# Second MLP product on one core: the last chunk's 42 rows, high and low half stacked in one tile, two matmuls in place of three

## The chip, the core and the metric

The kernel runs on one core of one Trainium2 chip. The metric is the device time of one execution in microseconds (us). The kernel before takes 3081.09 us, the median of three runs (3079.54 to 3083.18). The core's engines are named as in the profile: PE is TensorE (PEld its weight loads), DVE is VectorE, ACT is ScalarE, POOL is GpSimd, SP is SyncE, which issues the DMAs. Every engine runs its own instruction stream, and the streams meet at semaphores.

## The reference

The input x has shape (4, 2048, 256). Two blocks follow each other, each with a residual and layer norms:

```python
x = x + layernorm(attention(layernorm(x)))     # softmax over axis 1, full attention of each batch
x = x + layernorm(transformer(layernorm(x)))   # two layers, windows of 128 tokens
# one layer: x += local_attention(shift(x) @ wqkv, 8 heads of 64) @ wo
#            h  = layernorm(shift(x)) * g + b
#            a, g = split(h @ w1 + b1, 2)      # HID = 682 columns each
#            x += (a * gelu(g)) @ w2 + b2      # w2 is 682 x 256
```

The change concerns the last line, the product with w2. Its contraction runs over HID = 682 = 5 x 128 + 42 values.

## The kernel before

The function `phase_a` computes the first block (up to about 650 us of the profile). `phase_b` starts with a stage that loads and splits the weights (about 651 to 729 us) and then runs both layers as one stream of 128 windows of 128 tokens, 64 of layer 0 and 64 of layer 1. Each engine has a function `run(s, r, pairs, layer)` that issues its work of slot `s`; in a slot, different windows are in different steps. Most slots stand in two hardware loops of four slots, the first slots of each layer and the last ones are written out. The order of the work is written by hand in these functions; nothing reorders it.

The MLP is done for two windows at a time, a pair. In an even slot (`r % 2 == 0`) PE computes the product with w1 (L1000). ACT applies the gelu (L1101), DVE multiplies (L1238) and leaves `hid`, in 6 chunks of up to 128 hidden values (on the partitions) by 256 tokens. Only 42 partitions of the last chunk, number FULL = 5, are used. To get more than 16-bit precision out of 16-bit products, POOL splits each chunk: `hid_hl[:, 0]` is the value rounded to float16 (the high half, L1253), `hid_hl[:, 1]` the rest (the low half, L1255). It does four chunks at the end of the even slot and the last two in the odd slot, in the middle of its other work. w2 is split in the same way before the stream starts. In the odd slot PE computes the product with w2 (L1012): for each of two windows and each of 6 chunks three matmuls of 256 columns, given by `PARTS`: high by high, high by low, low by high. That is 36 matmuls a pair, and 64 pairs. The unused partitions of the last chunk hold zeros (L1338).

What stands around this on each engine:

- PE, after the w2 product, turns q and k of the next window (L903, L910), computes the qkv product (L925), then turns the softmax weights of the window before (L941, 16 transposes) and multiplies them with v (L953), then computes scores (L966), the output product (L979), and in even slots the w1 product (L1000). In an even slot L941 waits for `xpp` (L1156), DVE's reading of the w2 product. L953 waits for ACT's copies of the turned weights (L1068).
- DVE, in the odd slot, takes the scores (L1204), then normalises the 8 heads' weights (L1216), heads 0 to 3, then the low half of the next input (L1112), then heads 4 to 7. In the next slot come the low halves of q and k (L1181, L1183), the statistics of the layer norm (L1140, L1143), then `xpp` (L1156) and the rotary terms (L1125, L1126).
- POOL, in the odd slot: layer norm helpers (L1272 to L1277), the squares (L1281), the last two chunks of `hid_hl` (L1253, L1255), then qr and the sum for kr (L1289, L1291), inverse norms (L1295, L1297), kr (L1301), the inverse norm of q (L1305), xb (L1310), the low half of the layer norm's output (L1262), and in layer 1 the final sum (L1333). When the next slot is the first of a group of four, a mask copy (L1268) follows.
- ACT, in the even slot, makes the normalised input (L1039, L1041) from POOL's `shift2` (L1277), which comes from DVE's L1143, and only after it the copies L1068.

The constant `SECOND_REST` is 64, the first partition of the upper half of a tile.

Of the kernel before, what the change touches and what calls it, by code (L numbers as in the profile page):

```python
# [21 lines left out]
ALU = mybir.AluOpType  # L22
# [5 lines left out]
P = 128  # L28
# [4 lines left out]
LAYERS, HEADS, DH = 2, 8, 64  # L33
INNER = HEADS * DH
HP = HEADS // 2
HID = int(D * 4 * 2 / 3)
FULL = HID // P
REST = HID - FULL * P
HC = FULL + 1

W1_BLOCKS = 2 * FULL + 1
SECOND_REST = P // 2
# [20 lines left out]
LAST_SLOT = NT + 6  # L63
FILL_GROUPS = 2
PARTS = ((0, 0), (0, 1), (1, 0))
HID_EARLY = 4
W1_BANKS = (0, 1, 6, 3, 4, 5)
BANK_READ = {3: 3, 4: 4, 5: 7, 6: 8}
# [438 lines left out]
def phase_b(nc, w, consts, x2_dram, xs_dram, xp_dram, rot_dram, out):  # L507
# [9 lines left out]
    with ExitStack() as keep:  # L517
# [9 lines left out]
        w2 = sb("w2", [P, LAYERS, 2, HC, D], F16)  # L527
# [9 lines left out]
        with ExitStack() as ctx:  # L537
# [14 lines left out]
            w2_f = sb("w2_f", [P, LAYERS, HC, D])  # L552
# [4 lines left out]
            bias_sq, low = sb("bias_sq", [P, LAYERS]), sb("low", [P, 3, LAYERS])  # L557
# [8 lines left out]
            step, scale_ready, w1_hi, w2_hi, bias_added = sem("step"), sem("scale_ready"), sem("w1_hi"), sem("w2_hi"), sem("bias_added")  # L566
            loaded_mlp = sem("loaded_mlp")
            block = ctx.enter_context(nc.Block())
            DMAS_ROT, DMAS_MLP, DMAS = 1 + 6, LAYERS * 5 + 1, 4

            @block.sync
            def _(sp):
# [11 lines left out]
                for l in range(LAYERS):  # L584
                    sp.dma_start(w2_f[:, l, 0:FULL, :], w["w2"][l, 0:FULL * P, :].rearrange("(c p) d -> p c d", p=P)).then_inc(loaded_mlp, 16)
                    for first_block, first_row, half in ((0, 0, 0), (HC, SECOND_REST, HID)):
# [1 line left out]
                                     allow_slow_non_contiguous=True).then_inc(loaded_mlp, 16)  # L588
                        sp.dma_start(b1_f[first_row:first_row + REST, l, FULL:HC], w["b1"][l, half + FULL * P:half + HID].rearrange("(p c) -> p c", c=1),
                                     allow_slow_non_contiguous=True).then_inc(loaded_mlp, 16)  # L590
                sp.dma_start(w2_f[0:REST, :, FULL, :], w["w2"][:, FULL * P:HID, :].rearrange("l p d -> p l d")).then_inc(loaded_mlp, 16)

                sp.dma_start(rot_all[:, (LAYERS - 1) * WPB:LAYERS * WPB, :], consts["rot"]).then_inc(loaded_rot, 16)
                for n, name in enumerate(("q_scale", "k_scale")):
# [136 lines left out]
        with ExitStack() as ctx:  # L731
# [33 lines left out]
            hid = sb("hid", [P, HC, 2 * P])  # L765
            hid_hl = sb("hid_hl", [P, 2, HC, 2 * P], F16)
# [26 lines left out]
            w1_done, gelu_done, hid_ready, hid_hi, hid_lo = (sem(n) for n in ("w1_done", "gelu_done", "hid_ready", "hid_hi", "hid_lo"))  # L793
# [4 lines left out]
            vk_cleared = sem("vk_cleared")  # L798
# [88 lines left out]
            def _(pe):  # L887
# [7 lines left out]
                def run(s, r, pairs, layer):  # L895
# [88 lines left out]
                    j = pairs - 2  # L984
# [19 lines left out]
                    if r % 2 == 1 and in_range(2 * j):  # L1004

                        pe.wait_ge(hid_lo, HC * (j + 1))
                        if in_range(s - 1):
                            pe.wait_ge(scores_kept, HEADS * (s - 1) + BANK_READ[3])
                        for n in range(2):
                            for c in range(HC):  # L1010
                                for a, (hp, wp) in enumerate(PARTS):
                                    last = nc.tensor.matmul(ps[:, 3, n * D:(n + 1) * D], hid_hl[:, hp, c, n * P:(n + 1) * P],  # L1012
                                                            w2[:, ds(layer(2 * j), 1), wp, c, :],
                                                            start=(c == 0 and a == 0), stop=(c == HC - 1 and a == 2))
                        last.then_inc(w2_done, 1)

                transpose_hx(0, 0)
# [227 lines left out]
            def _(pool):  # L1245
                def hid_halves(j, first, end):

                    if in_range(2 * j):
                        wait(pool, w2_done, j)
                        for c in range(first, end):  # L1250
                            rows = slice(0, P if c < FULL else REST)
                            wait_apart(pool, hid_ready, HC * j + c + 1, passed_pool)
                            nc.gpsimd.tensor_copy(hid_hl[rows, 0, c, :], hid[rows, c, :]).then_inc(hid_hi, 1)  # L1253
                            pool.wait_ge(hid_hi, HC * j + c + 1)
                            nc.gpsimd.tensor_tensor(hid_hl[rows, 1, c, :], hid[rows, c, :], hid_hl[rows, 0, c, :], ALU.subtract).then_inc(hid_lo, 1)  # L1255

                def input_low(t):
                    if in_range(t):
# [76 lines left out]
                nc.gpsimd.memset(v[:], 0.0).then_inc(vk_cleared, 1)  # L1335
                nc.gpsimd.memset(kT[:].bitcast(F32), 0.0).then_inc(vk_cleared, 1)
                nc.gpsimd.memset(kT_low[:].bitcast(F32), 0.0).then_inc(vk_cleared, 1)
                nc.gpsimd.memset(hid_hl[:, :, FULL, :], 0.0).then_inc(vk_cleared, 1)  # L1338
                slots(pool, run)


# [57 lines left out]
```

## Time and profile before

| | |
|---|---|
| median of three runs | 3081.09 us |
| the profiled execution's own time | 3083.64 us |
| its span, first to last instruction | 3081.9 us |
| PE busy | 2908.2 us (94%) |
| PE weight loads busy | 2508.8 us (81%) |
| DVE busy | 2481.2 us (81%) |
| POOL busy | 2070.3 us (67%) |
| ACT busy | 2038.6 us (66%) |
| mean granted TensorE clock | 0.978 of full speed |

The profile is one execution. PE's busy time counts a matmul until its modelled end, so that matmuls overlap in it; the weight loads (PEld), of which there is one for each matmul, show better when PE had nothing to do. DVE's and POOL's instructions are shown with start and duration in us. An idle time in brackets is that of the engine just before the instruction, with what ended it. "Layer 0" in the stream is about 825 to 1995 us by the starts of the w2 products, "layer 1" what follows.

### The profile page before, as it was taken

The page shows a single profiled execution, that of the slowest core. Times are in us where ns is not written, and L with a number is a line of the kernel's source. Part 1 is how long each engine was busy: PE and PEld are TensorE (multiplying, and loading weights), DVE is VectorE, ACT ScalarE, POOL GpSimd, SP SyncE. Part 2 cuts the span into 40 slices and gives each one's busy share as a digit, 9 for nine tenths or more (in the row PEclk, how much of TensorE's full clock was granted, in tenths as well). Part 3 has the DMA queues.
Part 4 walks back from the last instruction along what each step waited for, and adds up shares of the span by engine and source line. Part 5 has one row for each costly group of instructions (what it writes and reads, how often), then busy time and mean ns, then how long its engine had stood idle before and what let it go on. Part 6 is the DMA issues. An engine that isn't in the chain of part 4 may idle for free. (4 is left out here: it accounts for less than half of the span.)

```text
span 3081.9 us, 81609 instructions
## 1 busy us (share of the span) xinstructions
PE 2908.2 (94%) x25720; PEld 2508.8 (81%) x25720; DVE 2481.2 (81%) x6734; ACT 2038.6 (66%) x4644; POOL 2070.3 (67%) x2807
## 2 busy tenths in 40 slices
PE   7999999963999999999999999999999999999996
PEld 4868676753888888888888888888888888888885
DVE  7989888746887888887888888888888888888884
ACT  6253534203777777777777777777777777777774
POOL 0323232124778878778777777888888888888885
PEclk9999999976999999999999999999999999999998
DMA  1211111151111111111111111222121112221221
GB/s 39 62 49 56 55 56 49 47 179 75 49 55 48 51 54 53 53 50 48 52 57 51 54 48 49 56 66 57 56 60 55 54 55 59 65 58 56 59 55 44
DMA packets 273029, 176.92 MB, mean 57 GB/s; under 512 B 95775, under 2 KB 270851, under 8 KB 272515
## 3 DMA queue, kind: packets, MB, share of 16 engines
q1 hardware_dynamic: 272898, 175.24, 19.4%
q8 instruction: 75, 1.23, 0.2%
q14 instruction: 56, 0.45, 0.1%
HBM read 103.82 MB, written 54.54 MB: 51 GB/s over the span
## 5 line engine op out<-in xcount | busy, mean ns | idle before, releaser
L1086 ACT ACTIVATE b_probs<-b_probs,b_negmax 128x256 f32<-128x256 f32 x1024 | 507.9, 498 | 77.2 <-DVE b_negmax L1204 76.5
L925 PE MATMUL b_ps<-b_wqkv,b_hT_hi 128*128 128x512 f32 x1536 | 499.1, 406 | 3.0 <-issue 2.0
L1000 PE MATMUL b_ps<-b_h2T,b_w 128*128 128x256 f16 x4224 | 473.7, 273 | 8.3 <-DMA b_h2T<-b_xh_hl 8.3
L1000 PEld LDWEIGHTS b_ps<-b_h2T,b_w 128*128 128x128 f16 x4224 | 414.0, 98 | 56.9 <-DMA b_h2T<-b_xh_hl 8.6
L1216 DVE TENSOR_SCALAR b_probs<-b_probs,b_rinv 128x256 f32<-128x256 f32 x1024 | 412.8, 466 | 9.0
L457 PE MATMUL a_ps<-a_xn_hl,a_E 128*128 128x256 f16 x3072 | 344.5, 273 | 8.8 <-DVE a_E L323 8.8
L457 PEld LDWEIGHTS a_ps<-a_xn_hl,a_E 128*128 128x128 f16 x3072 | 299.4, 98 | 44.2 <-ACT a_e L402 9.6
L925 PEld LDWEIGHTS b_ps<-b_wqkv,b_hT_hi 128*128 128x128 f32 x1536 | 283.4, 191 | 62.5 <-issue 2.4
L1204 DVE CUSTOM_DVE_ANT_0 b_probs<-b_ps,b_mask,b_rn 128x256 f32<-128x256 f32 x768 | 317.8, 480 | 0.0
L1173 DVE TENSOR_TENSOR b_oT<-b_ps,b_oT 128x512 fp32r<-128x512 f32 x128 | 88.6, 692 | 280.9 <-ACT b_oT L1077 280.9
L1068 ACT COPY b_probsT<-b_ps 128x512 f32<-128x512 f32 x512 | 261.2, 593 | 80.9 <-PE b_ps L941 80.8
L925 PE MATMUL b_ps<-b_wqkv,b_hT_lo 128*128 128x512 f32 x768 | 306.4, 399 | 0.0
L1255 POOL TENSOR_TENSOR b_hid_hl<-b_hid,b_hid_hl 128x256 f16<-128x256 f32 (+1 forms) x384 | 258.2, 673 | 30.9
L1012 PE MATMUL b_ps<-b_w,b_hid_hl 128*128 128x256 f16 x2304 | 261.9, 273 | 3.0 <-POOL b_hid_hl L1255 3.0
L941 PEld LDWEIGHTS b_ps<-b_ident_f,b_probs 128*128 128x128 f32 x2048 | 230.6, 142 | 39.9 <-issue 20.4
L941 PE MATMUL b_ps<-b_ident_f,b_probs 128*128 128x128 f32 x2048 | 247.5, 274 | 13.8 <-DVE b_xpp L1156 12.4
L953 PE MATMUL b_ps<-b_probsT,b_v 128*64 128x128 f32 x4096 | 256.3, 278 | 3.4 <-ACT b_probsT L1068 1.1
L1012 PEld LDWEIGHTS b_ps<-b_w,b_hid_hl 128*128 128x128 f16 x2304 | 224.8, 98 | 28.9 <-POOL b_hid_hl L1255 3.2
L953 PEld LDWEIGHTS b_ps<-b_probsT,b_v 128*64 128x64 f32 x4096 | 219.0, 136 | 33.4 <-ACT b_probsT L1068 19.9
L1101 ACT ACTIVATE b_gl<-b_ps,b_b,b_w_unit 128x256 f32<-128x256 f32 (+1 forms) x384 | 203.0, 562 | 52.8 <-PE b_ps L1000 39.5
L1305 POOL TENSOR_TENSOR b_rn<-b_ss_min,b_mhalf 128x8 f32<-128x8 f32 x128 | 233.3, 1822 | 0.0
L1238 DVE SCALAR_TENSOR_TENSOR b_hid<-b_ps,b_b1a,b_gl 128x256 f32<-128x256 f32 (+1 forms) x384 | 177.6, 481 | 62.7 <-ACT b_gl L1101 62.7
(164 smaller groups left out, 6830.7 us busy)
## 6 DMA issues: line engine op xcount, KB each, us to landing
b_hx<-xs_dram SPq DMA_DIRECT2D x256, 64.0 KB, 1.9
b_rot<-rot_dram SPq DMA_DIRECT2D x128, 128.0 KB, 2.1
b_xr<-xs_dram SPq DMA_DIRECT2D x128, 128.0 KB, 2.1
xp_dram<-b_xp SPq DMA_DIRECT2D x128, 128.0 KB, 1.7
b_h<-xp_dram SPq DMA_DIRECT2D x256, 64.0 KB, 1.8
a_x_res<-in_L_attn_x_dram SPq DMA_DIRECT2D x64, 128.0 KB, 2.2
x_dram<-a_x SPq DMA_DIRECT2D x64, 128.0 KB, 1.7
xs_dram<-a_xo SPq DMA_DIRECT2D x64, 128.0 KB, 1.8
```

The costliest lines, as they stand in the source:

```text
L457: last = nc.tensor.matmul(ps[:, bank, 0:D], E[:, j, a, i * P:(i + 1) * P], xn_hl[:, b % 2, j, c, :], start=(j == 0 and a == 0 and c == 0), ...
L925: last = nc.tensor.matmul(ps[:, bank, :], hT[:, k, :], wqkv[:, ds(layer(s), 1), part, k, bank * INNER:(bank + 1) * INNER], start=(k == 0 a ...
L941: last = nc.tensor.transpose(ps[:, 3 + p, n * P:(n + 1) * P], probs[:, 2 * p + n // 2, (n % 2) * P:(n % 2 + 1) * P], ident_f[:])
L953: last = nc.tensor.matmul(ps[h * DH:(h + 1) * DH, 7, p * P:(p + 1) * P], v[:, window, (2 * p + h) * DH:(2 * p + h + 1) * DH], probsT[:, p, ...
L1000: last = nc.tensor.matmul(ps[:, bank, half * 2 * P:(half + 1) * 2 * P], w1[:, ds(layer(2 * j), 1), wp, k, first:first + P], h2T[:, hp, k, ...
L1012: last = nc.tensor.matmul(ps[:, 3, n * D:(n + 1) * D], hid_hl[:, hp, c, n * P:(n + 1) * P], w2[:, ds(layer(2 * j), 1), wp, c, :], start=(c ...
L1068: nc.scalar.copy(probsT[:, p, :], ps[:, 3 + p, :]).then_inc(pT_kept, 1)
L1086: nc.scalar.activation(probs[:, h, :], probs[:, h, :], ACT.Exp, bias=negmax[:, h:h + 1], scale=-1.0, accum_out=rowsum[:, h:h + 1]).then_in ...
L1204: nc.vector.tensor_tensor_reduce(probs[:, h, :], head_scores(h), which, rn[:, (r - 1) % 2, h:h + 1], ABOVE_ALL, ALU.add, ALU.min, negmax[: ...
L1216: nc.vector.tensor_scalar(probs[:, h, :], probs[:, h, :], rinv[:, h:h + 1], None, ALU.mult).then_inc(probs_ready, 1)
L1255: nc.gpsimd.tensor_tensor(hid_hl[rows, 1, c, :], hid[rows, c, :], hid_hl[rows, 0, c, :], ALU.subtract).then_inc(hid_lo, 1)
L1305: nc.gpsimd.tensor_tensor(rn[:, r % 2, :], ss_min[:, 0:HEADS], mhalf[:, 0:HEADS], ALU.pow).then_inc(rn_ready, 1)
```

## The change

The last chunk's high half stays on partitions 0 to 41 of `hid_hl[:, 0, FULL]`. Its low half is no longer written to `hid_hl[:, 1, FULL]` but to partitions 64 to 105 of the same tile `hid_hl[:, 0, FULL]`. The last 42 rows of w2 are loaded twice, to partitions 0 to 41 and to 64 to 105, by a DMA more. One matmul over the stacked tile and the weights' high half then gives high by high plus low by high, and one over the weights' low half gives high by low plus low by low, a product that was left out before. The last chunk takes two matmuls a window (`REST_PARTS`) in place of three. POOL, which writes both halves of the stacked tile, gets a wait for its own last write of the pair before it goes on. The clearing of the tile (one memset before the stream) covers half as much.

```diff
--- before.py
+++ after.py
@@ -63,6 +63,7 @@
 LAST_SLOT = NT + 6
 FILL_GROUPS = 2
 PARTS = ((0, 0), (0, 1), (1, 0))
+REST_PARTS = ((0, 0), (0, 1))
 HID_EARLY = 4
 W1_BANKS = (0, 1, 6, 3, 4, 5)
 BANK_READ = {3: 3, 4: 4, 5: 7, 6: 8}
@@ -566,7 +567,7 @@
             step, scale_ready, w1_hi, w2_hi, bias_added = sem("step"), sem("scale_ready"), sem("w1_hi"), sem("w2_hi"), sem("bias_added")
             loaded_mlp = sem("loaded_mlp")
             block = ctx.enter_context(nc.Block())
-            DMAS_ROT, DMAS_MLP, DMAS = 1 + 6, LAYERS * 5 + 1, 4
+            DMAS_ROT, DMAS_MLP, DMAS = 1 + 6, LAYERS * 5 + 2, 4
 
             @block.sync
             def _(sp):
@@ -588,7 +589,8 @@
                                      allow_slow_non_contiguous=True).then_inc(loaded_mlp, 16)
                         sp.dma_start(b1_f[first_row:first_row + REST, l, FULL:HC], w["b1"][l, half + FULL * P:half + HID].rearrange("(p c) -> p c", c=1),
                                      allow_slow_non_contiguous=True).then_inc(loaded_mlp, 16)
-                sp.dma_start(w2_f[0:REST, :, FULL, :], w["w2"][:, FULL * P:HID, :].rearrange("l p d -> p l d")).then_inc(loaded_mlp, 16)
+                for first_row in (0, SECOND_REST):
+                    sp.dma_start(w2_f[first_row:first_row + REST, :, FULL, :], w["w2"][:, FULL * P:HID, :].rearrange("l p d -> p l d")).then_inc(loaded_mlp, 16)
 
                 sp.dma_start(rot_all[:, (LAYERS - 1) * WPB:LAYERS * WPB, :], consts["rot"]).then_inc(loaded_rot, 16)
                 for n, name in enumerate(("q_scale", "k_scale")):
@@ -1008,10 +1010,10 @@
                             pe.wait_ge(scores_kept, HEADS * (s - 1) + BANK_READ[3])
                         for n in range(2):
                             for c in range(HC):
-                                for a, (hp, wp) in enumerate(PARTS):
+                                for a, (hp, wp) in enumerate(PARTS if c < FULL else REST_PARTS):
                                     last = nc.tensor.matmul(ps[:, 3, n * D:(n + 1) * D], hid_hl[:, hp, c, n * P:(n + 1) * P],
                                                             w2[:, ds(layer(2 * j), 1), wp, c, :],
-                                                            start=(c == 0 and a == 0), stop=(c == HC - 1 and a == 2))
+                                                            start=(c == 0 and a == 0), stop=(c == HC - 1 and a == 1))
                         last.then_inc(w2_done, 1)
 
                 transpose_hx(0, 0)
@@ -1252,7 +1254,10 @@
                             wait_apart(pool, hid_ready, HC * j + c + 1, passed_pool)
                             nc.gpsimd.tensor_copy(hid_hl[rows, 0, c, :], hid[rows, c, :]).then_inc(hid_hi, 1)
                             pool.wait_ge(hid_hi, HC * j + c + 1)
-                            nc.gpsimd.tensor_tensor(hid_hl[rows, 1, c, :], hid[rows, c, :], hid_hl[rows, 0, c, :], ALU.subtract).then_inc(hid_lo, 1)
+                            low = hid_hl[rows, 1, c, :] if c < FULL else hid_hl[SECOND_REST:SECOND_REST + REST, 0, c, :]
+                            nc.gpsimd.tensor_tensor(low, hid[rows, c, :], hid_hl[rows, 0, c, :], ALU.subtract).then_inc(hid_lo, 1)
+                            if c == FULL:
+                                pool.wait_ge(hid_lo, HC * (j + 1))
 
                 def input_low(t):
                     if in_range(t):
@@ -1335,7 +1340,7 @@
                 nc.gpsimd.memset(v[:], 0.0).then_inc(vk_cleared, 1)
                 nc.gpsimd.memset(kT[:].bitcast(F32), 0.0).then_inc(vk_cleared, 1)
                 nc.gpsimd.memset(kT_low[:].bitcast(F32), 0.0).then_inc(vk_cleared, 1)
-                nc.gpsimd.memset(hid_hl[:, :, FULL, :], 0.0).then_inc(vk_cleared, 1)
+                nc.gpsimd.memset(hid_hl[:, 0, FULL, :], 0.0).then_inc(vk_cleared, 1)
                 slots(pool, run)
 
 
```

On PE, in the odd slots of the hardware loop, these rows stand around the w2 product before (`b_ps` is the PSUM tile, `b_w` the split w2, `b_hid_hl` the split hidden values, `b_qr` and `b_kr` the rotated q and k; in brackets the semaphores waited for):

```order
L979 MATMUL b_ps<-b_wo,b_oT 128x256 [waits b_v_kept,b_oT_lo]
L979 MATMUL b_ps<-b_wo,b_oT 128x256 x11
L892 MATMUL b_ps<-b_ident_f,b_hx 128x128 [waits b_oT_lo,b_hx_loaded]
L892 MATMUL b_ps<-b_ident_f,b_hx 128x128
L1012 MATMUL b_ps<-b_w,b_hid_hl 128x256 [waits b_scores_kept,b_hid_lo]
L1012 MATMUL b_ps<-b_w,b_hid_hl 128x256 x35
L903 MATMUL b_ps<-b_ident_f,b_qr 128x128 [waits b_xp_ready,b_v_kept,b_qr_ready]
```

And these in the changed kernel, whose lines are numbered two higher here:

```order
L981 MATMUL b_ps<-b_wo,b_oT 128x256 [waits b_v_kept,b_oT_lo]
L981 MATMUL b_ps<-b_wo,b_oT 128x256 x11
L894 MATMUL b_ps<-b_ident_f,b_hx 128x128 [waits b_oT_lo,b_hx_loaded]
L894 MATMUL b_ps<-b_ident_f,b_hx 128x128
L1014 MATMUL b_ps<-b_w,b_hid_hl 128x256 [waits b_scores_kept,b_hid_lo]
L1014 MATMUL b_ps<-b_w,b_hid_hl 128x256 x33
L905 MATMUL b_ps<-b_ident_f,b_qr 128x128 [waits b_xp_ready,b_v_kept,b_qr_ready]
```

Two matmuls of 36 are gone; the neighbours and all waits of PE are the same.

On POOL, in the same odd slots, the rows around the last two chunks before:

```order
L1281 TENSOR_TENSOR b_sq<-b_sq 128x16x32 [waits b_k_sq]
L1253 CAST b_hid_hl<-b_hid 128x256 [waits b_w2_done,b_hid_ready]
L1255 TENSOR_TENSOR b_hid_hl<-b_hid,b_hid_hl 128x256 [waits b_hid_hi]
L1253 CAST b_hid_hl<-b_hid 42x256 [waits b_hid_ready]
L1255 TENSOR_TENSOR b_hid_hl<-b_hid,b_hid_hl 42x256 [waits b_hid_hi]
L1289 TENSOR_TENSOR b_qr<-b_t 128x512 [waits b_qT_done,b_q_terms]
L1291 TENSOR_TENSOR b_t<-b_t 128x512 [waits b_k_terms]
```

And in the changed kernel:

```order
L1286 TENSOR_TENSOR b_sq<-b_sq 128x16x32 [waits b_k_sq]
L1255 CAST b_hid_hl<-b_hid 128x256 [waits b_w2_done,b_hid_ready]
L1258 TENSOR_TENSOR b_hid_hl<-b_hid,b_hid_hl 128x256 [waits b_hid_hi]
L1255 CAST b_hid_hl<-b_hid 42x256 [waits b_hid_ready]
L1258 TENSOR_TENSOR b_hid_hl<-b_hid,b_hid_hl 42x256 [waits b_hid_hi]
L1294 TENSOR_TENSOR b_qr<-b_t 128x512 [waits b_qT_done,b_q_terms,b_hid_lo]
L1296 TENSOR_TENSOR b_t<-b_t 128x512 [waits b_k_terms]
```

The operations are the same; the one after the last low half now also waits for `b_hid_lo`, the semaphore that this low half itself raises when it is done. The wait stands between the two as an instruction of POOL's sequencer.

## Rows read from the trace of the kernel before

**Rows 1.** Busy us of each engine in a stretch of layer 0 and of layer 1

```profile
1000.00:1500.00 500.00, 500.00 (x4604) 445.84 (x4601) 407.15 (x1194) 383.42 (x936) 394.58 (x515) 1.00 0.18 51
2000.00:2500.00 500.00, 493.79 (x4482) 432.96 (x4481) 422.08 (x1205) 387.40 (x931) 428.24 (x575) 1.00 0.21 59
```

**Rows 2.** Waits of the weight loads, 1995 to 2976 us: total us, times, longest

```profile
PEld b_ps L941 <- issue: 20.4, 26, 0.8
```

**Rows 3.** Timeline of a layer 1 pair, weight loads and a copy: start, us, engine

```profile
2031.31 3.92 PEld L1012 LDWEIGHTS b_ps<-b_w,b_hid_hl 128*128 128x128 f16 x36
2039.95 0.19 PEld L925 LDWEIGHTS b_ps<-b_wqkv,b_hT_lo 128*128 128x128 f32 x1
2040.92 1.73 PEld L941 LDWEIGHTS b_ps<-b_ident_f,b_probs 128*128 128x128 f32 x16 [0.78 <-issue]
2042.33 0.56 ACT L1068 COPY b_probsT<-b_ps 128x512 f32<-128x512 f32 x1
2042.94 0.31 PEld L953 LDWEIGHTS b_ps<-b_probsT,b_v 128*64 128x64 f32 x6 [0.29 <-ACT b_probsT L1068]
```

**Rows 4.** Timeline of the same pair, DVE (narrow windows keep single instructions apart)

```profile
2033.20 0.35 DVE L1216 TENSOR_SCALAR b_probs<-b_probs,b_rinv 128x256 f32<-128x256 f32 x1
...
2035.06 0.83 DVE L1216 TENSOR_SCALAR b_probs<-b_probs,b_rinv 128x256 f32<-128x256 f32 x1
...
2036.49 1.37 DVE L1216 TENSOR_SCALAR b_probs<-b_probs,b_rinv 128x256 f32<-128x256 f32 x1
...
2039.92 0.88 DVE L1156 SCALAR_TENSOR_TENSOR b_xpp<-b_ps,b_w_unit,b_xb 128x256 f32<-128x256 f32 x2 [0.20 <-issue]
```

**Rows 5.** Timeline of the same pair, POOL

```profile
2023.92 0.26 POOL L1277 TENSOR_SCALAR b_shift<-b_mv,b_rstd 128x1 f32<-128x1 f32 x1 [0.21 <-POOL b_rstd L1275]
...
2026.46 0.39 POOL L1253 CAST b_hid_hl<-b_hid 42x256 f16<-42x256 f32 x1
2026.93 0.66 POOL L1255 TENSOR_TENSOR b_hid_hl<-b_hid,b_hid_hl 42x256 f16<-42x256 f32 x1
2027.56 1.26 POOL L1289 TENSOR_TENSOR b_qr<-b_t 128x512 f32<-128x512 f32 x1
...
2032.27 1.04 POOL L1301 TENSOR_TENSOR b_kr<-b_t,b_rn_k 128x512 f32<-128x512 f32 x1
2033.27 1.92 POOL L1305 TENSOR_TENSOR b_rn<-b_ss_min,b_mhalf 128x8 f32<-128x8 f32 x1
2035.01 0.72 POOL L1310 TENSOR_TENSOR b_xb<-b_xp,b_b 128x256 f32<-128x256 f32 x1
...
2036.38 1.33 POOL L1333 TENSOR_TENSOR b_fin<-b_fin,b_x 128x512 f32<-128x512 f32 x1
```

**Rows 6.** Timelines of another window in layer 0's last part: POOL, then DVE

```profile
1960.51 1.04 POOL L1301 TENSOR_TENSOR b_kr<-b_t,b_rn_k 128x512 f32<-128x512 f32 x1
...
1961.38 0.35 DVE L1216 TENSOR_SCALAR b_probs<-b_probs,b_rinv 128x256 f32<-128x256 f32 x1
```

**Rows 7.** Timelines of two layer 0 pairs, ACT's copies and PE's weight loads

```profile
1507.04 0.19 PEld L925 LDWEIGHTS b_ps<-b_wqkv,b_hT_lo 128*128 128x128 f32 x1
1507.27 1.90 PEld L941 LDWEIGHTS b_ps<-b_ident_f,b_probs 128*128 128x128 f32 x16
1508.59 1.05 ACT L1068 COPY b_probsT<-b_ps 128x512 f32<-128x512 f32 x2
1509.34 0.74 PEld L953 LDWEIGHTS b_ps<-b_probsT,b_v 128*64 128x64 f32 x14 [0.17 <-ACT b_probsT L1068]
...
1543.83 1.04 ACT L1068 COPY b_probsT<-b_ps 128x512 f32<-128x512 f32 x2
1544.79 0.20 PEld L953 LDWEIGHTS b_ps<-b_probsT,b_v 128*64 128x64 f32 x4 [0.17 <-issue]
```

**Rows 8.** Timeline of the weight stage: a DMA issue of SP, and ACT

```profile
666.61 0.39 SPq L591 DMA_DIRECT2D p_w_f<-in_L_ffn_w_dram  x1
...
690.12 2.75 ACT L648 CAST b_wqkv<-p_wqkv_f 128x3072 fp32r<-128x3072 f32 x1 [125.85 <-DMA p_wqkv_f<-in_L_ffn_wqkv_dram]
```

## The prediction

> **What bounds the kernel now.** I read the busy times by stretch first [rows 1]. In layer 0 PE is busy all the time and POOL, DVE and ACT are not; in layer 1 PE does 4482 matmuls in 500 us where layer 0 has 4604, and POOL and DVE are busier. So the two layers have different limits, and a saving on PE must be followed in each. The waits of the weight loads come next [rows 2]: in layer 1, L941 stood still for 0.8 us in 26 of about 30 pairs, 20.4 us in all; no such row is there for layer 0. Last I followed one pair of each layer through the timelines, from the w2 product to the two places where PE meets the other engines again: L941, which waits for DVE's `xpp`, and L953, which waits for ACT's first copy L1068, and that stands behind DVE's statistics and POOL's `shift2`.
>
> In layer 1, `xpp` ends at 2039.92 + 0.88 = 2040.80 and L941 starts at 2040.92; the load before it stood at 2039.95 [rows 3, 4]. In layer 0 the same two loads are 0.23 apart [rows 7], so PE loses 0.97 - 0.23 = 0.74 us there. L953 starts 0.05 us after the first copy ends (2042.33 + 0.56 = 2042.89, then 2042.94), so it is bound too [rows 3]. Both ends come from DVE. Its last normalisation runs 2036.49 to 2037.86, 1.37 us, and POOL's L1333 runs 2036.38 to 2037.71 [rows 4, 5]: DVE's instruction ends 0.15 us after POOL's. The second of that four does the same, 2035.06 to 2035.89, with L1310 ending at 2035.73. Alone such an instruction takes 0.35. So DVE's L1216 is held up by a POOL instruction that started before it, and in layer 1 DVE's chain to `xpp` hangs on the end of POOL's chain. POOL works without a gap from L1281 to L1333 in the odd slot, so its chain is the bound of this part, and the w2 product lies beside it.
>
> In layer 0 nothing follows L1262 but the short mask copy, and DVE is in time. The copy starts at 1508.59 in one pair and its first of two ends 0.56 later, 1509.15; L953 starts at 1509.34. With the 0.05 from above, PE could come 0.13 us earlier before L953 waits. In the other kind of pair (1543.83 + 0.56 = 1544.39, then 1544.79) it is 0.35 [rows 7]. The kinds alternate, since the mask copy is there in every second pair: 17 of the 33 pairs of layer 0 have the small room, 16 the large one.
>
> **The change part by part.** Two matmuls of 36 go. The loads of the 36 span 3.92 us [rows 3]; less the last load's own 0.10 that is 3.82 over 35, 0.109 each, so 0.218 a pair and 64 x 0.218 = 14.0 us if PE bound everything. It does not: in layer 1 (27 pairs with the 0.8 us stall or a like one) PE only arrives earlier at a wait, and gets nothing.
>
> POOL's new wait adds to its chain. Today L1289 starts at 2027.56, 0.03 before L1255 ends (2026.93 + 0.66) [rows 5]. With the wait it starts after that end. Two rows price a wait for one's own last result: L1255 starts 0.08 after the L1253 whose result it waits for, and L1277, whose wait stands as an instruction of its own before it, starts 0.21 after (the bracket) [rows 5]. The new wait stands as its own instruction too, with one more behind it (the wait for `qT_done`), so I take 0.25; the bounds are 0.08 and 0.29. With the 0.03 of overlap lost, POOL's chain comes 0.28 us later (0.11 to 0.32). Behind the waiting instruction stand all of POOL's operations up to L1333. PE's turning of kr (L910) stands behind the whole w2 product, which starts at 2031.31 and takes 3.9 us [rows 3], so L1301, ended at 2033.31, has 1.9 us of cover there.
>
> Not covered is DVE. L1301 ends at 2033.31, 0.11 after DVE's first L1216 starts at 2033.20, and that one still takes 0.35 [rows 4, 5]. At another window L1301 ends at 1961.55, 0.17 after L1216 starts at 1961.38, and it still takes 0.35 [rows 6]. By the rule read off above (DVE ends 0.15 after POOL) the hold-up begins when POOL's end passes 0.20 after DVE's start. 0.11 + 0.28 = 0.39 passes it by 0.19. So the first normalisation, and the seven behind it back to back, come 0.19 later in layer 1; in layer 0, where L1301 ends about 0.10 after, 0.18. L1305 and L1310 on POOL stand in the same relation to DVE as before (L1305 starts 0.04 before L1301 ends, in both), so that the same four blocks follow, all shifted: 0.19 us on `xpp` and on the copies. In layer 1 the pair grows by that.
>
> The Trainium skill (SBUF — State Buffer, Who interferes with whom) has a rule for this that speaks against the change: a DVE `tensor_scalar` in a two-port mode and a GpSimd instruction exclude each other, and who comes first holds the port pair for the whole instruction. The trace agrees on who waits; it doesn't on the whole instruction, for L1216 at 2033.20 isn't held up by the last 0.11 us of L1301 [rows 4, 5]. By that rule the full 0.28 would pass on to DVE, and layer 1 would lose 27 x 0.28 = 7.6 us in place of the 5.1 below.
>
> That POOL's low half now goes to other partitions than it reads I cost at nothing, for want of a row with such a shift. Its bounds are 0 and, by the nearest row taken once more, 0.66 us a pair [rows 5]. The added DMA costs SP one issue, 0.39 us, ahead of the load of wqkv, for whose landing ACT had idled at 690.12 [rows 8]; its 84 KB are little beside. I take +0.4 (0.2 to 0.5). The smaller clearing is beside other starts: nothing. The last pairs (4, with no full stream behind them) give up to 0.218 each: -0.7.
>
> **The sum**, made against the profiled execution (3083.64 us, span 3081.9), which is 2.55 above the median 3081.09; the difference is carried to the median.
> - Layer 0, 16 pairs with room 0.35: DVE's chain takes 0.18 of it, PE gains 0.17 each: -2.7.
> - Layer 0, 17 pairs with room 0.13: the chain comes 0.18 later, 0.05 past the room: +0.9.
> - Layer 1, 27 pairs: 27 x 0.19 = +5.1.
> - Last pairs -0.7, DMA +0.4.
> Together +3.0: 3086.6 for such an execution, 3084.1 against the median, 0.1% slower. With the wait at its lower bound, 0.11, POOL's end is 0.22 after DVE's start and DVE is pushed 0.02: layer 0 gives 16 x 0.218 + 17 x 0.11 = 5.4, layer 1 +0.5, sum -5.2. With 0.32 the push is 0.23: 16 x -0.12 + 17 x 0.10 + 27 x 0.23 - 0.3 = +5.7. The likeliest case's own range is 3078 to 3088. A measurement of this kernel can hardly tell 0.2%, 6.2 us, from no change: 3075 to 3087.
>
> **The rivals.**
> - The wait is cheap: -5.2, 3076. For it: L1255's 0.08. Against: the wait stands alone, like L1277's.
> - PE's saving comes through whole: -14.0 + 0.4, 3067.5. For it: PE is busy 100% of layer 0. Against: L941 and L953 in layer 1, which hang on DVE and not on PE.
> - The collision turns over. L1310 starts at 2035.01, only 0.05 before DVE's second normalisation of the four [rows 4, 5]. If POOL came some 0.1 us later against DVE there, DVE would go first, its third would wait for L1310, its fourth for L1262, and none for L1333: the last one would end 0.15 after L1262, at 2036.83 and not at 2037.86, 1.03 earlier. PE would then be bound in layer 1 as in layer 0: it gets back 0.74 at L941, about 0.15 at L953 and its 0.218, 1.1 us x 27 = 30, and 7 in layer 0: 3044. Against it: both engines are pushed together from L1301 on, so their distance should stay.
> - Slower: the low half written to partitions 64 to 105 takes POOL longer, at the same place in its chain. Each 0.3 us more delays L1301 by 0.3, and now nothing takes it up, so `xpp` and the copies come 0.3 later in each pair: 60 x 0.3 = 18 on top: 3102. It decides from about 0.05 us on (60 x 0.05 = 3, past 0.2%). For it: POOL's chain is what layer 1 hangs on. Against: it is the same arithmetic on as many values, and no row shows a cost of the place written to.
>
> **How the numbers follow.** Chances: the push as worked out 0.55; the cheap wait 0.12; the whole saving 0.08; the turned collision 0.08; the slower write 0.17. I predict the first, 3084. The range leaves out the turned collision and half of the slower write's upper part: 3067 to 3096. Faster by over 0.2%: 0.08 + 0.08 and a third of the cheap wait and a little of the first, 0.22. Slower by over 0.2%: 0.17 and some of the first case, 0.24. Within: 0.54.
>
> **What would show it.** In the profile after, 34 loads of the w2 product span 3.70 us. POOL's qr starts 0.25 us after the last low half ends (0.08 says cheap wait), and that low half takes 0.66 (more says the slower write). In layer 1, DVE's first normalisation takes 0.54 and not 0.35, the last one still 1.37; if the last takes some 0.76, the collision has turned over. PE's stall before L941 grows from 0.74 to some 1.15. Wrong would be a layer 1 pair shorter than before, or `xpp` not later against the scores.

## The result and the profile after

The changed kernel takes 3091.66 us (median of 7 runs, 3086.15 to 3093.84); the kernel before, on the same chip, 3082.20 (7 runs, 3079.54 to 3083.18). The ratio is 1.0030, 95% interval 1.0019 to 1.0041: slower by 5.9 to 12.6 us, where 3.0 were forecast (9.5 by the medians). The profiled execution of the changed kernel took 3091.81 us with a span of 3090.0, so it stands 8.17 above that of before.

In the profile after, lines of TensorE, ACT and DVE bear numbers higher by 2, and those of POOL by 2 to 5: L1012 is L1014, L1216 is L1218, L1255 (the low half) L1258, L1289 (qr) L1294, L1301 (kr) L1306, L1333 (the final addition) L1338.

The same two stretches as in [rows 1]: stretch, length, then busy us and count of PE, PEld, DVE, ACT, POOL, then clock, DMA share, GB/s.

```profile
1000.00:1500.00 500.00, 498.69 (x4564) 440.92 (x4563) 408.20 (x1189) 382.28 (x936) 393.41 (x514) 1.00 0.18 52
2000.00:2500.00 500.00, 488.26 (x4414) 426.12 (x4413) 423.86 (x1204) 384.49 (x926) 424.70 (x570) 1.00 0.21 58
```

In layer 0 PE is no longer busy all the time. Its matmuls are fewer in both stretches because two in each pair are gone, so their count says nothing of the pace; the length of a pair does. I took it from the first weight load of one w2 product to that of the next, for every pair, in all the profiles of this study. "Even" and "odd" are the two kinds of pair, counted from 0 at the first product; in layer 0 the even ones are those with the larger room of [rows 7]. The lengths are those of a steady pair; the medians of each kind agree with them to 0.02 us. The last two columns are the sums of the first 33 pairs (layer 0) and of the next 27 (layer 1).

```
us                              layer 0         layer 1         33 pairs  27 pairs
                                even   odd      even   odd
before                          35.43  35.46    36.28  36.36    1169.9    980.7
after                           35.40  35.62    36.54  36.55    1171.7    986.9
wait alone, 36 matmuls          35.43  35.62    36.53  36.54    1172.8    986.5
34 matmuls, no wait             35.22  35.45    36.28  36.36    1167.3    980.6
after, other order              35.22  35.46    36.29  36.36    1166.7    980.8
after, addition held            35.43  35.65    35.54  35.54    1172.4    959.6
before, addition held           35.43  35.44    35.43  35.43    1170.5    956.8
after, order and hold           35.22  35.46    35.25  35.34    1166.8    953.2
before, order and hold          35.43  35.43    35.43  35.43    1169.9    956.7
before, two waits               35.75  35.96    36.80  36.88    1182.5    994.6
```

So of the 8.17 us between the two profiles +1.8 arose in layer 0 and +6.2 in layer 1. The rest, -2.7 ahead of the first product and +2.9 behind the 60th pair, can't be laid to the change: over the ten profiles the first product starts between 821.2 and 825.2 us, in no order that goes with what the kernels do, and the length of the last 70 to 73 us goes with TensorE's granted clock. The last w2 product shows it, of before and then of after (columns as above):

```profile
3068.70:3072.90 4.20, 4.11 (x36) 3.44 (x36) 0.03 (x1) 0.00 (x0) 1.19 (x1) 1.00 0.41 125
```

```profile
3074.20:3081.00 6.80, 6.76 (x34) 4.72 (x34) 0.00 (x0) 0.00 (x0) 1.26 (x1) 0.56 0.24 77
```

With granted clock 1.00 (the 2.4 GHz level) 36 matmuls took 4.11 us, with 0.56 (most of it at the 1.2 GHz level) 34 took 6.76. In the last 20 us of either kernel PE is busy for 8. Five of the eight experiments below have the lower clock in their last product too, two of them with 36 matmuls and nothing stacked. All four kernels with the stacked tile have it, in one profile each, so a tie to the change is not excluded; but the experiment "The wait alone" shows the whole loss without the stacked tile.

**Waits of the weight loads**, engine, line, what ended them, then total us, times, longest: layer 1 (1994 to 2981), which answers to [rows 2], and layer 0 (825 to 1990) in after, then layer 0 in before.

```profile
PEld b_ps L943 <- issue: 30.7, 26, 1.2
...
PEld b_ps L927 <- DVE b_qT_low L1183: 6.3, 26, 0.5
...
PEld b_ps L955 <- ACT b_probsT L1070: 13.5, 56, 0.4
...
PEld b_ps L955 <- issue: 2.7, 10, 0.7
```

```profile
PEld b_ps L953 <- ACT b_probsT L1068: 7.1, 42, 0.2
PEld b_ps L953 <- issue: 4.4, 24, 0.5
```

The stall in front of L943 grew from 20.4 to 30.7 us; in layer 0 the waits at the loads behind the copies grew from 7.1 + 4.4 = 11.5 to 13.5 + 2.7 = 16.2. (The same view of after has 2.8 us of waits in front of L943, 0.2 in each of 13 pairs, where before had none. The waits at the copies stand behind them.)

**A pair of layer 1**, the weight loads, in answer to [rows 3] (start, us):

```profile
2249.94 3.70 PEld L1014 LDWEIGHTS b_ps<-b_w,b_hid_hl 128*128 128x128 f16 x34
...
2258.47 0.19 PEld L927 LDWEIGHTS b_ps<-b_wqkv,b_hT_lo 128*128 128x128 f32 x1
2259.83 1.73 PEld L943 LDWEIGHTS b_ps<-b_ident_f,b_probs 128*128 128x128 f32 x16 [1.17 <-issue]
2261.85 0.42 PEld L955 LDWEIGHTS b_ps<-b_probsT,b_v 128*64 128x64 f32 x8 [0.29 <-ACT b_probsT L1070]
```

The product is 0.22 us shorter, and L943 follows the load before it by 1.36 us where it was 0.97. What PE gained it waits away, and 0.17 more; some 0.11 stands further up, where L927 waits for DVE's `qT_low`. POOL of the same pair, in answer to [rows 5]:

```profile
2245.09 0.39 POOL L1255 CAST b_hid_hl<-b_hid 42x256 f16<-42x256 f32 x1
2245.56 0.67 POOL L1258 TENSOR_TENSOR b_hid_hl<-b_hid,b_hid_hl 42x256 f16<-42x256 f32 x1
2246.53 1.29 POOL L1294 TENSOR_TENSOR b_qr<-b_t 128x512 f32<-128x512 f32 x1 [0.30 <-POOL b_hid_hl L1258]
...
2251.25 1.04 POOL L1306 TENSOR_TENSOR b_kr<-b_t,b_rn_k 128x512 f32<-128x512 f32 x1
...
2255.28 1.34 POOL L1338 TENSOR_TENSOR b_fin<-b_fin,b_x 128x512 f32<-128x512 f32 x1
```

The low half still takes 0.67 us, now that it goes to partitions 64 to 105. Behind it stands an idle time of 0.30 that was not there. Over the whole trace it is counted as 13.4 us in 54 times, 0.25 each. And DVE, in answer to [rows 4] and the DVE row of [rows 6], the first and the last of the eight normalisations:

```profile
2251.82 0.61 DVE L1218 TENSOR_SCALAR b_probs<-b_probs,b_rinv 128x256 f32<-128x256 f32 x1
...
2255.39 1.39 DVE L1218 TENSOR_SCALAR b_probs<-b_probs,b_rinv 128x256 f32<-128x256 f32 x1
```

The first took 0.35 and takes 0.61 (0.54 in odd pairs), and ends 0.15 after L1306 does (2252.43 against 2252.29). The last is held up as long as before, by L1338.

### The profile page after: what moved, and what is told of

The parts are those of the page before. It is cut to its first block and busy times, and to the rows that moved or that the text cites. A ratio compares the mean times of both kernels' runs of the same rounds, so it can differ in the third digit from the quotient of the medians.

```text
span 3090.0 us, 81381 instructions
## 1 busy us (share of the span) xinstructions
PE 2901.9 (94%) x25592; PEld 2491.1 (81%) x25592; DVE 2491.8 (81%) x6734; ACT 2037.5 (66%) x4644; POOL 2067.8 (67%) x2807
## 5 line engine op out<-in xcount | busy, mean ns | idle before, releaser
L927 PE MATMUL b_ps<-b_wqkv,b_hT_hi 128*128 128x512 f32 x1536 | 500.2, 407 | 3.0 <-issue 1.9
L1218 DVE TENSOR_SCALAR b_probs<-b_probs,b_rinv 128x256 f32<-128x256 f32 x1024 | 423.4, 475 | 9.1
L927 PEld LDWEIGHTS b_ps<-b_wqkv,b_hT_hi 128*128 128x128 f32 x1536 | 281.0, 191 | 66.5 <-DVE b_qT_low L1183 6.3
L927 PE MATMUL b_ps<-b_wqkv,b_hT_lo 128*128 128x512 f32 x768 | 306.3, 399 | 0.0
L1258 POOL TENSOR_TENSOR b_hid_hl<-b_hid,b_hid_hl 128x256 f16<-128x256 f32 (+1 forms) x384 | 258.3, 673 | 31.0
L943 PEld LDWEIGHTS b_ps<-b_ident_f,b_probs 128*128 128x128 f32 x2048 | 229.6, 142 | 52.9 <-issue 33.5
L943 PE MATMUL b_ps<-b_ident_f,b_probs 128*128 128x128 f32 x2048 | 247.4, 274 | 25.6 <-DVE b_xpp L1158 24.4
L1014 PE MATMUL b_ps<-b_w,b_hid_hl 128*128 128x256 f16 x2176 | 250.8, 274 | 3.0 <-POOL b_hid_hl L1258 3.0
L1014 PEld LDWEIGHTS b_ps<-b_w,b_hid_hl 128*128 128x128 f16 x2176 | 213.8, 98 | 28.8 <-POOL b_hid_hl L1258 3.2
```

The source lines that it names most:

```text
L927: last = nc.tensor.matmul(ps[:, bank, :], hT[:, k, :], wqkv[:, ds(layer(s), 1), part, k, bank * INNER:(bank + 1) * INNER], start=(k == 0 a ...
L943: last = nc.tensor.transpose(ps[:, 3 + p, n * P:(n + 1) * P], probs[:, 2 * p + n // 2, (n % 2) * P:(n % 2 + 1) * P], ident_f[:])
L1218: nc.vector.tensor_scalar(probs[:, h, :], probs[:, h, :], rinv[:, h:h + 1], None, ALU.mult).then_inc(probs_ready, 1)
L1258: nc.gpsimd.tensor_tensor(low, hid[rows, c, :], hid_hl[rows, 0, c, :], ALU.subtract).then_inc(hid_lo, 1)
```

## The experiments

In all of them, theory A is the push: POOL's wait delays kr, kr holds up DVE's normalisations, and PE waits for what stands behind those. Each ratio is against the kernel before, run beside the experiment: 3082.27 us (16 runs) for the wait alone, the two matmuls alone and the two kernels with the final addition held, 3083.75 us (15 runs) for the other four. The rows of each experiment bear the line numbers of its own kernel.

The expectations use other names for some work. The "rounding copy" on VectorE is a normalisation, L1216. The "bias product" is L941 where a wait of about 1 us stands ahead of it, and L953 where ACT's four copies feed its loads. GpSimd's "sum and rounding" of a pair are its instructions from L1289 on, and the normalisations that these hold up.

**The wait alone.** The kernel before and:

```diff
                             nc.gpsimd.tensor_tensor(hid_hl[rows, 1, c, :], hid[rows, c, :], ...).then_inc(hid_lo, 1)
+                            if c == FULL:
+                                pool.wait_ge(hid_lo, HC * (j + 1))
```

> The kernel before with GpSimd's added wait alone, the 36 matmuls kept. Theory A (the wait pushes the rounding copy of layer 1 and the copies of layer 0 through the lock of GpSimd and VectorE): layer 1 gains nothing and pays 27 x 0.19 = +5.1 us; in layer 0 the 17 odd pairs, which have no room at the bias product's loads, pay 0.18 each (+3.1), the 16 even ones 0 to 0.03 each (+0 to +0.5); sum +8 to +9, 3090 to 3092 us, so about as slow as the changed kernel or slower by some 1 us; in layer 1 VectorE's first rounding copy after the change of scores takes 0.84 in place of 0.83 and starts 0.2 later in the pair. Theory B (the wait is cheap, the changed kernel is slower for another cause: the load placed twice, the stacked tile's write, or a state of the clock at the end): within 0.1%, 3080 to 3085 us.

Measured: 3093.11 us (6 runs), ratio 1.0033 (1.0021 to 1.0046), 1 us above the expected range. That is the changed kernel's loss, with nothing stacked, nothing loaded twice and 36 matmuls. POOL and DVE of a layer 1 pair look as they do in the changed kernel:

```profile
2249.31 0.67 POOL L1255 TENSOR_TENSOR b_hid_hl<-b_hid,b_hid_hl 42x256 f16<-42x256 f32 x1
2250.28 1.29 POOL L1291 TENSOR_TENSOR b_qr<-b_t 128x512 f32<-128x512 f32 x1 [0.30 <-POOL b_hid_hl L1255]
...
2255.00 1.04 POOL L1303 TENSOR_TENSOR b_kr<-b_t,b_rn_k 128x512 f32<-128x512 f32 x1
...
2255.58 0.61 DVE L1216 TENSOR_SCALAR b_probs<-b_probs,b_rinv 128x256 f32<-128x256 f32 x1
```

Theory B falls. Layer 0 pays +0.16 in odd pairs and nothing in even ones, as expected; layer 1 +0.21 in the mean and not 0.19. The normalisation of 0.83 us is the sixth of the eight, which again takes 0.83 and starts 0.26 us later in even pairs and 0.18 in odd ones.

**Two matmuls alone.** The kernel before and:

```diff
-                                for a, (hp, wp) in enumerate(PARTS):
+                                for a, (hp, wp) in enumerate(PARTS if c < FULL else PARTS[:2]):
...
-                                                            start=(c == 0 and a == 0), stop=(c == HC - 1 and a == 2))
+                                                            start=(c == 0 and a == 0), stop=(c == HC - 1 and a == 1))
```

> The kernel before with two matmuls for the last chunk and no wait; it leaves out the product of the low half of the last chunk's 42 rows with the weights' high half. Theory A (the copies, not TensorE, set a pair's length): layer 1 0 us in 27 pairs, with the wait before the bias product's weight load longer by 0.2 us; layer 0 0.15 to 0.2 gained in each of 16 even pairs where the fourth copy leaves that room, and 0 in the 17 odd ones: -2.4 to -3.2 us, and 0.2 at the last pair, so 3078 to 3080 us. Rival B (TensorE sets the length, and the added wait ate the gain elsewhere): 0.22 in each of 60 pairs, -13 us, 3069 us.

Measured: 3078.57 us (11 runs), ratio 0.9990 (0.9981 to 0.9999); layer 1 unchanged, even pairs of layer 0 shorter by 0.21, odd ones by 0.01. Both halves of theory A hold: 14 us less work of PE is worth 3.7 us by the medians (0.3 to 5.9), 2.7 by the sums of the 60 pairs.

**Another order on POOL.** The same stacked tile, but chunk 5's low half is computed between chunk 4's two halves, so that the wait which it needs takes the place of one that was there (high 4, high 5, wait, low 5, wait, low 4):

```diff
-                        for c in range(first, end):
+                        step = end - first if end == HC else 1
+                        for c0 in range(first, end, step):
+                            for c in range(c0, c0 + step):
...
+                            pool.wait_ge(hid_hi, HC * j + c0 + step)
+                            for c in reversed(range(c0, c0 + step)):
...
+                                if c == FULL:
+                                    pool.wait_ge(hid_lo, HC * j + HC - 1)
```

> The changed kernel with GpSimd's last five instructions of a pair's halves in another order: high of chunk 4, high of chunk 5, wait, low of chunk 5, wait, low of chunk 4. The stacked tile and the 34 matmuls are kept, and there are two waits on an own result, as in the kernel before. Theory A (one wait on an own result more is all that the change cost): the pair's sum and rounding are back at the times of before, layer 1 at 36.3 us a pair, layer 0 at 35.22 and 35.46, as with two matmuls and no wait: 3077 to 3081 us, 11 to 14 below the changed kernel. Rival B (the stacked write, the second load of the weights' part or the different addresses cost something themselves): 3085 us or more.

Measured: 3081.74 us (11 runs), ratio 0.9993 (0.9984 to 1.0002): 10 us below the changed kernel. Pairs are as long as with two matmuls and no wait, to 0.01 us, so the stacked write and the doubled load cost nothing in them. The median lies 0.7 us above the expected range, but the kernel before, too, took 1.5 us more beside it than beside the two matmuls alone, and the two ratios agree. The wait behind the low half of chunk 5 now stands ahead of the low half of chunk 4. It leaves 0.08 us there (2240.65 to 2240.73), in every pair, where it left 0.22 to 0.30 ahead of qr, and qr follows the last low half without a gap again:

```profile
2239.98 0.67 POOL L1262 TENSOR_TENSOR b_hid_hl<-b_hid,b_hid_hl 42x256 f16<-42x256 f32 x1
2240.73 0.67 POOL L1262 TENSOR_TENSOR b_hid_hl<-b_hid,b_hid_hl 128x256 f16<-128x256 f32 x1
2241.36 1.27 POOL L1298 TENSOR_TENSOR b_qr<-b_t 128x512 f32<-128x512 f32 x1
```

The change as it is, but without its wait, was not run, so no run here shows what the wait is needed for.

**Two waits.** The kernel before, with a wait behind the low half of chunk 4 as well:

```diff
+                            if c >= FULL - 1:
+                                pool.wait_ge(hid_lo, HC * j + c + 1)
```

> The kernel before, 36 matmuls, with a wait on the own result behind the low half of chunk 4 and of chunk 5. Theory A (each wait delays the pair's sum and the rounding by 0.2 us; layer 0's copies have 0.21 us of room in even pairs and 0.02 in odd ones): layer 1 at 36.53 + 0.21 = 36.74 us a pair, layer 0 at about 35.58 (even) and 35.80 (odd): 3082.3 + 27 x 0.42 + 16 x 0.15 + 17 x 0.34 = 3102 us. Rival B (the second wait falls into idle time, ahead of the wait for VectorE's chunk 5 or of the pair's q terms): 3093 to 3096 us.

Measured: 3110.97 us (5 runs), ratio 1.0087 (1.0073 to 1.0101), a miss by 9 us, above both. The second wait costs more than the first: with both, pairs grow by 0.52 in layer 1, where one wait made 0.21. POOL and DVE of an even pair of layer 1:

```profile
2257.03 0.39 POOL L1253 CAST b_hid_hl<-b_hid 42x256 f16<-42x256 f32 x1 [0.24 <-POOL b_hid_hl L1255]
2257.50 0.66 POOL L1255 TENSOR_TENSOR b_hid_hl<-b_hid,b_hid_hl 42x256 f16<-42x256 f32 x1
2258.39 1.29 POOL L1291 TENSOR_TENSOR b_qr<-b_t 128x512 f32<-128x512 f32 x1 [0.23 <-POOL b_hid_hl L1255]
...
2263.13 1.04 POOL L1303 TENSOR_TENSOR b_kr<-b_t,b_rn_k 128x512 f32<-128x512 f32 x1
...
2263.45 0.87 DVE L1216 TENSOR_SCALAR b_probs<-b_probs,b_rinv 128x256 f32<-128x256 f32 x1
```

Each wait is 0.23 to 0.24 of idle time. The expectation took twice the first one's net effect; but in that one kr first had to use up the time for which it could run on beside the first normalisation without holding it up (0.09 us by [rows 4, 5]), and the second wait finds none. In even pairs kr ends 0.60 later against the start of the first normalisation than in before, in place of 0.35 with one wait, and that normalisation lasts 0.87 in place of 0.61 and 0.35: the second 0.25 or 0.26 is passed on whole.

**The final addition held.** The same two lines, in the changed kernel and in the kernel before, ahead of POOL's last instruction of the pair:

```diff
                         pool.wait_ge(x2_loaded, 16 * (f + 1))
+                        if in_range(s - 1):
+                            pool.wait_ge(probs_ready, HEADS * s)
                         nc.gpsimd.tensor_tensor(fin[:], fin[:], x2[:], ALU.add).then_inc(fin_ready, 1)
```

> The changed kernel, with GpSimd's final addition of the pair held till VectorE has done its eight normalisations. Theory A (in layer 1 the last rounding copy on VectorE takes 1.39 in place of 0.34 us because this addition has the port shared with VectorE, and all copies behind it are late by this, of which TensorE waits 1.36 us ahead of the bias product): the copy takes 0.34 to 0.40 us, the wait ahead of the product falls to 0.3 to 0.4, and layer 1 gains 27 x 1.0 = 27 us: 3060 to 3068 us. Rival B (GpSimd's own chain sets the pair: the addition comes later by 1 to 3 us, and what stands behind it on GpSimd is late by the same): 0 to +30 us, 3090 to 3120.

> The same hold of the final addition in the kernel before. Theory A: layer 1 gains 27 x (0.97, the most that TensorE waits there) = up to 26 us, 3055 to 3062 us; and since room then appears at the bias product, the changed kernel with this hold is no longer slower than the kernel before with it but even, or faster by up to 27 x 0.2 = 5 us. Rival B (GpSimd's chain sets the pair): 3081 to 3110 us, and the changed kernel stays 9 us behind.

Measured: 3061.81 us for the changed kernel (ratio 0.9933, 0.9919 to 0.9946) and 3060.89 for the one before (0.9930, 0.9916 to 0.9943). Both times lie in the expected ranges. DVE, POOL and PE of the changed kernel's layer 1:

```profile
2250.38 0.34 DVE L1218 TENSOR_SCALAR b_probs<-b_probs,b_rinv 128x256 f32<-128x256 f32 x1
...
2250.80 1.31 POOL L1340 TENSOR_TENSOR b_fin<-b_fin,b_x 128x512 f32<-128x512 f32 x1 [0.49 <-DVE b_probs L1218]
...
2253.78 1.73 PEld L943 LDWEIGHTS b_ps<-b_ident_f,b_probs 128*128 128x128 f32 x16 [0.27 <-issue]
```

POOL stands idle for 0.49 us ahead of its addition; DVE's last normalisation falls from 1.39 to 0.34, PE's stall from 1.17 to 0.27, and a pair of layer 1 from 36.55 to 35.54. In the kernel before with this line layer 1 runs at 35.43, as fast as layer 0: 36 matmuls, and PE is the bound. What the second expectation says of the change is shown in part. The two medians are 0.9 us apart, with intervals of 4 us to either side. But the pairs of the changed kernel stay longer, 35.65 against 35.44 in odd ones of layer 0 and 35.54 against 35.43 in layer 1, 4.7 us in all 60. So in these two profiles the hold alone doesn't make the change pay.

**Order and hold together**, with the change and (then with no wait behind a low half, for it needs none there) without it:

> The same order, and the final addition held till VectorE has done its normalisations. Theory A: layer 1 is bound by TensorE alone, at 35.43 - 0.22 = 35.21 to 35.3 us a pair, layer 0 as in the run with the order alone: 3061 - 27 x (0.13 to 0.22) - 3.4 = 3052 to 3054 us, faster than every kernel so far. Rival B (another bound, GpSimd's chain or a copy, stands within 0.2 us of TensorE in layer 1): 3057 to 3061 us.

> The kernel before with the same order (it needs no wait behind the low half of chunk 5, so one wait on an own result fewer than before) and the held addition, 36 matmuls. Theory A (TensorE bounds both layers once the copies have room): as the hold alone, 3058 to 3062 us, layer 1 at 35.43 a pair, layer 0 at 35.43 in both kinds of pair. Rival B (the shorter chain on GpSimd shortens pairs by itself): 3055 us or less.

Measured: 3053.16 us with the change (4 runs, 3052.04 to 3054.01; ratio 0.9901, 0.9886 to 0.9916), the fastest kernel of this case; 3059.79 without it (ratio 0.9921, 0.9908 to 0.9935). Both lie in theory A's ranges. So with the order and the hold the two matmuls are worth 6.6 us, about half of the 14 that PE has less to do. By pairs: 3.2 in layer 0 and 3.5 in layer 1. In layer 1 theory A's 35.21 was not quite reached, 35.25 and 35.34: part of rival B is true, for PE then waits for the copies. Layer 1 (1995 to 2955) of this kernel:

```profile
PEld b_ps L955 <- ACT b_probsT L1070: 8.9, 52, 0.3
PEld b_ps L943 <- issue: 0.3, 1, 0.3
```

## Why the prediction was right, and where it was not

- **PE's saving.** The unstalled product is 0.218 us shorter, as worked out, and layer 1 gets nothing of it (34 matmuls without the wait: 980.6 against 980.7 us). Right.
- **The wait's price.** Taken as 0.25 by the row of an instruction that stands apart; 0.25 is the mean over 54. kr came 0.27 us later in odd pairs of layer 1 and 0.35 in even ones, against 0.28. The cheap wait (0.08) falls.
- **The push on DVE.** The first normalisation was to take 0.54, and takes 0.54 in odd pairs, 0.61 in even ones; `xb`, `xpp` and the copies come 0.19 to 0.20 later in odd pairs of layer 1, 0.26 to 0.28 in even ones, and 0.17 to 0.19 in both kinds of layer 0. PE's stall before L941, forecast at 1.15, is 1.36 - 0.23 = 1.13. The mechanism is right; 27 pairs gave +6.2 us in place of +5.1, since one push was taken for both kinds. Why the wait leaves 0.30 us in even pairs of layer 1 and 0.22 in all others stays open.
- **The Trainium skill's rule** (SBUF — State Buffer, Who interferes with whom), that who comes first holds the port pair for the whole instruction, would have passed 0.28 on. Here the first wait's delay lost 0.08 to 0.09 on the way and the second's none, so in these runs the rule holds but for the first piece of overlap.
- **The slower write** to partitions 64 to 105, the rival with the highest chance: 0.67 us as before. **The turned collision** did not come: the last normalisation takes 1.39. **The DMA** of +0.4 cannot be seen: the stage ahead of the pairs was 2.7 us shorter, within what it differs between runs.
- **The step that failed is layer 0's room.** The sum had "16 pairs with room 0.35 [...] PE gains 0.17 each: -2.7" and "17 pairs with room 0.13 [...] 0.05 past the room: +0.9", together -1.8. It came to +1.8: even pairs gained 0.03 and odd ones lost 0.16. The prediction read the room at the first of ACT's four copies, where L953 starts. But each copy feeds eight of the 32 loads, and they come 0.48 us apart while eight loads pass in 0.44, so PE runs up to the later ones. What counts is the room at the fourth.

The fourth copy and the loads behind it, in the odd pair of [rows 7] in before: ACT, then PEld.

```profile
1510.01 0.60 ACT L1068 COPY b_probsT<-b_ps 128x512 f32<-128x512 f32 x1
...
1510.67 0.42 PEld L953 LDWEIGHTS b_ps<-b_probsT,b_v 128*64 128x64 f32 x8
```

The copy ends at 1510.61 and the 25th load starts 0.06 later, as close behind as L953's start to the first copy (0.05): room 0.00 and not 0.13. In the even pair of [rows 7] the fourth copy ends at 1545.25 + 0.60 = 1545.85, and the loads run through without a stop from the 23rd, at 1545.94; the 25th is at 1546.05: room 0.15 at that load and not 0.35.

```profile
1545.25 0.60 ACT L1068 COPY b_probsT<-b_ps 128x512 f32<-128x512 f32 x1
...
1545.94 0.58 PEld L953 LDWEIGHTS b_ps<-b_probsT,b_v 128*64 128x64 f32 x10
```

After the change that even pair waits at it too; the fourth copy, which ends at 1544.43, and the loads from the 25th on, in after:

```profile
1543.83 0.60 ACT L1070 COPY b_probsT<-b_ps 128x512 f32<-128x512 f32 x1
...
1544.48 0.42 PEld L955 LDWEIGHTS b_ps<-b_probsT,b_v 128*64 128x64 f32 x8
```

The eight loads behind a wait then pass 0.05 faster than they did unheld (0.28 against 0.33 from the start of the 25th to that of the last), which gives 0.20 for the even pair. The experiments agree with this: with two matmuls fewer alone, even pairs gained 0.21 and odd ones 0.01; with the wait alone, even ones lost 0.00 and odd ones 0.16; with both, 0.18 - 0.21 = -0.03 and 0.18 - 0.02 = +0.16. (The 0.02 is read back from these runs; the timeline gives 0.00.) With rooms of 0.21 and 0.02 in place of 0.35 and 0.13 the prediction's sum gives +2.2 for the 33 pairs, and with the measured +6.2 for layer 1 and its own last terms 8 us in all, inside what the runs show (9.5, interval 5.9 to 12.6). The prediction also had the counts of the two kinds the wrong way round: 17 pairs are even and 16 odd, which makes the +2.2 a +2.1.

What decided the sign was therefore right for its reason. The size was a third of the true one, mostly because the gain set against the loss was not there (3.6 us of the 6.5 missed); 1.1 us come from the larger push in layer 1, and the rest is within what the runs differ by.

## What to carry to other kernels

A wait on an engine for which TensorE itself hardly ever stands idle can cost more than the matmuls that it saves: follow the waiting engine's chain to each place where it holds up the next one. If an engine must wait for its own result, try other places for the wait: here one cost 0.08 us and another 0.22 to 0.30. Where a producer delivers in pieces, read the room at the last piece, not at the first. And if an engine is held up by another's instruction whose result nobody needs yet, hold that one back: an idle time of 0.5 us on POOL gave back 1.0 us a pair.

## What the runs showed of the hardware

- A DVE `tensor_scalar` instruction that starts while a GpSimd instruction runs ends 0.15 us after that one: 0.34 us became 1.39 beside an addition of 1.34, and was 0.34 again when the addition came later. It is not held up when the GpSimd instruction ends 0.11 us after its start (0.35 us). A delay of 0.35 us on POOL came out as 0.26 on DVE, the next 0.25 in full.
- A GpSimd wait for its own last result left 0.22 to 0.30 us idle ahead of qr, 0.24 more ahead of the high half of chunk 5 where a second one stood, but 0.08 ahead of the low half of chunk 4 in the other order. What makes the difference is not shown.
- Writing 42 partitions to other ones than are read costs a GpSimd subtraction of 42x256 no time (0.66 to 0.67 us in both cases).
- The last w2 product, 34 or 36 matmuls, took 3.9 to 4.1 us in the four profiles where the granted clock stayed at 1.00 through it, and 5.2 to 6.8 us in the six where it had fallen before it or fell in it.
